# Expert loop on TensorE: one expert load per chunk, small matmuls moved inside a layer, branch prefetch hints

## Time and profile before

| what | us |
| --- | --- |
| median of 3 runs | 583.89 |
| lowest and highest of them | 580.96, 586.48 |
| the profiled execution, its own time | 583.43 |
| the span of that execution in the profile | 581.7 |
| PE busy | 569.2 (98%) |
| DVE, ACT, POOL busy | 409.2, 262.7, 177.6 |

### The profile page before, as it was taken

One profiled execution on the slowest core, in us unless ns is written; L12 is line 12 of the kernel. 1 busy time (PEld: TensorE's weight loads), 2 busy tenths in 40 slices (PEclk: granted clock), 3 DMA queues, 4 the chain that ended last, 5 costly groups with the idle time before them and its releaser, 6 DMA issues.

```text
span 581.7 us, 17023 instructions
## 1 busy us (share of the span) xinstructions
PE 569.2 (98%) x5107; PEld 501.2 (86%) x5108; DVE 409.2 (70%) x1093; ACT 262.7 (45%) x576; POOL 177.6 (31%) x529
## 2 busy tenths in 40 slices
PE   9999999999999999999999999899999998999995
PEld 5888888885889999999999999799999996866874
DVE  5969996767846686777577688755756554568766
ACT  6666757622344343435343343343435342546360
POOL 0270000000663435352524323335242500189000
PEclk9999999999999999999999999999999998999999
DMA  8712254101001223220000000000000000192322
GB/s 266 258 76 72 79 174 145 56 1 38 2 1 32 81 103 117 83 102 38 2 2 3 2 2 3 2 3 2 3 1 3 2 4 5 30 366 81 110 101 87
DMA packets 28479, 36.92 MB, mean 63 GB/s; under 512 B 4762, under 2 KB 24115, under 8 KB 28132
## 3 DMA queue, kind: packets, MB, share of 16 engines
q1 hardware_dynamic: 28292, 35.57, 18.6%
q0 software_dynamic: 96, 0.20, 0.1%
HBM read 27.30 MB, written 8.53 MB: 62 GB/s over the span
## 4 chain that ended last, share of the span: by engine, by line
PE 96%; issue 1%; DVE 1%; ACT 0%; POOL 0%; POOLq 0%; DVEq 0%
PE ps_hidden L1168 43%; PE ps_out L1196 42%; PE ps_hidden L598 4%; PE ps_hidden L647 1%; PE ps_out L618 1%; PE ps_turn L1202 1%; PE ps_out L1242 1%; PE ps_out L610 1%; PE ps_turn L631 1%; PE ps_small L631 1%; DVE X L788 1%; DVE ytmp L871 0%; PE ps_turn L1249 0%; PE ps_small L1246 0%; ACT hbuf L533 0%
## 5 line engine op out<-in xcount | busy, mean ns | idle before, releaser
L1196 PE MATMUL ps_out<-hbuf,W 128*128 128x242 f16 (+2 forms) x2304 | 250.7, 269 | 0.0
L1196 PEld LDWEIGHTS ps_out<-hbuf,W 128*128 (+1 forms) x2304 | 224.4, 98 | 18.8 <-issue 0.2
L1741 POOL COPY xs<-X 128x88 f16 x352 | 126.4, 408 | 288.5 <-PE ps_hidden L1168 179.2
L1038 ACT ACTIVATE h<-ps_hidden,b 128x242 f32<-128x242 f32 (+1 forms) x384 | 155.5, 465 | 78.8 <-PE ps_hidden L1168 78.8
L1168 PE MATMUL ps_hidden<-xs,W 128*128 128x242 f16 x1536 | 165.8, 269 | 2.1 <-issue 2.1
L1168 PEld LDWEIGHTS ps_hidden<-xs,W 128*128 x1536 | 150.4, 98 | 12.8 <-issue 2.9
L1347 DVE TENSOR_TENSOR hbuf<-h,hbuf 128x484 f16<-128x484 f32 (+2 forms) x192 | 129.8, 676 | 7.5
L1628 DVE SCALAR_TENSOR_TENSOR acc<-ytmp,wrow,acc 128x44 f32 (+1 forms) x352 | 65.8, 260 | 94.7 <-ACT ytmp L1129 90.5
L1345 DVE CAST hbuf<-h 128x484 f16<-128x484 f32 (+2 forms) x192 | 84.9, 442 | 17.8 <-ACT h L1038 16.9
L1168 PE MATMUL ps_hidden<-X,W 128*128 128x256 f16 (+1 forms) x768 | 90.3, 279 | 2.7 <-issue 2.7
L1168 PEld LDWEIGHTS ps_hidden<-X,W 128*128 128x128 f16 x768 | 75.5, 99 | 15.7 <-issue 3.8
(11 more groups left out here) (294 smaller groups left out, 305.3 us busy)
## 6 DMA issues: line engine op xcount, KB each, us to landing
stage<-in_ew SPq DMA_DIRECT2D x16, 512.0 KB, 3.8
stage<-in_xR SPq DMA_DIRECT2D x8, 512.0 KB, 3.9
moved_rows<-stage SPq DMA_DIRECT2D x8, 512.0 KB, 2.6
X<-moved_rows SPq DMA_DIRECT2D x8, 512.0 KB, 10.0
out_rows<-X SPq DMA_DIRECT2D x16, 256.0 KB, 2.2
W<-in_xT SPq DMA_DIRECT2D x7, 512.0 KB, 9.2
W<-in_fw SPq DMA_DIRECT2D x1, 2304.0 KB, 11.8
W<-in_sw SPq DMA_DIRECT2D x4, 256.0 KB, 3.4
```

The costliest lines, as they stand in the source:

```text
L1038: i = nc.scalar.activation(h32[:, j, k * size:(k + 1) * size], ps1[j][:, k * size:(k + 1) * size], ACT.Gelu_apprx_tanh, bias=b1[:, bass.ds ...
L1196: mm = pe.matmul(out, w2(e, wp, hb, db), h, start=(n == 0), stop=(n == 3 * HB - 1))
L1741: i = nc.gpsimd.tensor_copy(xs[:, parity, :, j * SEG:(j + 1) * SEG], X[:, :, bass.ds(cols[j], SEG)])
```

## The change

On TensorE only:

- `hidden_expert` gets the expert as an argument. Each step reads one expert, and the register of the chunk before is passed on to `output`, which no longer reads it again.
- `output` has a hook `between`, which is called between its two halves.
- `pack` is no longer put behind step 20 but between the two halves of the output layer of that step.
- The count is read after step 15, one parity after step 16, the other after step 17, in place of all three after step 20.
- The nest of `If` becomes an explicit chain of `br_cmp` with bodies `chunk_24`, `chunk_25` and so on. Each step from 23 on computes `min(limit - (r + 1), 1)` in a register between the two halves of its output layer and marks there a prefetch hint for the branch at its end. The register is 1 when there is a next chunk and 0 when the branch will leave. All exits go to the label `chunks_done`.

```diff
-            def hidden_expert(r, parity):
+            def hidden_expert(r, parity, e):
                 pe.wait_ge(x_staged, r + 1)
-                hidden(r + R0, expert_of(r), lambda xp, db: xs[:, parity, 2 * xp + db, 0:RC], RC)
-
-            def output(g, e, parity, size=CH):
+                hidden(r + R0, e, lambda xp, db: xs[:, parity, 2 * xp + db, 0:RC], RC)
+
+            def output(g, e, parity, size=CH, between=None):
...
                 for db in range(DB):
+                    if db == 1 and between is not None:
+                        between()
...
-            def step(r, parity):
-                hidden_expert(r, parity)
-                output(r + (R0 - 1), expert_of(r - 1), 1 - parity, RC)
+            more = pe.alloc_register("more_chunks")
+
+            def step(r, before, between=None):
+
+                e = expert_of(r)
+                hidden_expert(r, r % 2, e)
+                output(r + (R0 - 1), before, (r - 1) % 2, RC, between)
                 if r == 14:
                     key()
                 if r == 18:
                     place()
-                if r == 20:
-                    pack()
-
-            last, parity, other = expert_loops(pe, 1, step)
+                return e
+
+            def tab_value(at):
+                return pe.value_load(tab[0:1, NR * ROW + at:NR * ROW + at + 1], min_val=0, max_val=1)
+
+            e = first_expert
+            for r in range(1, NRMIN - 1):
+                e = step(r, e, pack if r == 20 else None)
+                if r == 15:
+                    count = chunk_count(pe)
+                    limit = pe.to_reg(count)
+                if r == 16:
+                    parity = tab_value(1)
+                if r == 17:
+                    other = tab_value(3)
+
+            def chunks_from(r, before):
+
+                hint = []
+
+                def chunk_ahead():
+                    pe.reg_alu(more, limit, r + 1, ALU.subtract)
+                    pe.reg_alu(more, more, 1, ALU.min)
+                    hint.append(pe.mark_branch_hint_location(more))
+
+                e = step(r, before, chunk_ahead if r + 1 < NR else None)
+                if r + 1 < NR:
+                    pe.br_cmp(limit, r + 1, f"chunk_{r + 1}", "chunks_done", "IS_GT").branch_hint(hint[0])
+                    with nc.body(f"chunk_{r + 1}", valid_engines=[mybir.EngineType.PE]):
+                        chunks_from(r + 1, e)
+
+            chunks_from(NRMIN - 1, e)
+            pe.br("chunks_done")
+            nc.switch_bb("chunks_done")
+            last = count - 1
```

More of the change, by code:

```diff
@@ L1261, in _ @@
             pe.wait_ge(r_split, 4 * E)
-            hidden_expert(0, 0)
+            first_expert = expert_of(0)
+            hidden_expert(0, 0, first_expert)
             output(NS1 - 1, SH, 1)
```

## The result

| what | before | after |
| --- | --- | --- |
| median us | 584.34 (4 runs) | 575.61 (4 runs) |
| lowest and highest | 580.96, 586.48 | 574.51, 576.93 |
| ratio, 95% interval | | 0.9868, 0.9834 to 0.9903 |
| profiled execution, its span | 583.43, 581.7 | 576.93, 575.2 |

The changed kernel is 1.3% faster; 575.2 us was forecast, in a range of 572.6 to 579.3.

What follows compares the result with a forecast made beforehand. PE was taken as the bound, with gains only in its waits for its own sequencer and the slow clock behind them. 3.98 + 0.43 + 4.30 = 8.7 us off 583.43 gave 574.7, stated as 575.2 us, range 572.6 to 579.3.

Steps and rivals of the forecast that it cites:

- What bounds the kernel: Whole kernel: PE is busy 98% of the span; no matmul is removed, so gains come from its waits, the largest 4.9 us.
- Step 20: From `pack` to the next output layer: 9.44 us become 5.46, a gain of 3.98 us, 2.3 gap and 1.7 clock.
- The conditional chunks: Eight chunks from 406.11 us: one 0.65 us read less, 0.3 us for the hint, PE bound again; gain 0.43 us.
- The end of the loop: Leaving branch of 3.56 us: hint 2.5 us ahead plus 1.8 us lead hide it, no clock drop; gain 4.30 us.
- last branch well under 1 us: Sign that the forecast is right: the branch leaving the loop, 3557 ns before, takes well under 1 us.
- What hangs on the end of the loop: All after the loop moves with its end; VectorE's chunk 21 splits finish 3.6 us early, off the path.
- A: Rival at the loop's end: the hint starts nothing, gap 1.9 us, time 578.5 us, or 577.1 without clock drop; chance 0.25.
- B: Rival in the eight conditional chunks: the hint fetches the far block instead of the next; costs 25 us, time 605; chance 0.04.
- C: Rival in the conditional chunks: read or hint is dearer, hint 1 us or more, time near 580; chance with the rest 0.09.

Runs made afterwards that it cites:

- the two kernels that undo one half each: The changed kernel with `pack` put back behind step 20, 576.75 us; the changed kernel with the three reads put back behind step 20, 577.84 us.
- the last version: The changed kernel with the hint at the top of each step and three unread 512-column matmuls in a PE wait near the end; 575.19 us, ratio 0.9835.
- the two that lost it: The changed kernel with each output layer reading its expert again, 586.78 us; the changed kernel with later PE code shifted by 94 instructions, 580.05 us.
- the late hint: The changed kernel with the hint in the middle of the output layer's second half, 12 matmuls before the branch instead of 24; 579.01 us.
- the shifted one: The changed kernel with 50 small matmuls added to the warm-up and 3 large ones removed, moving later PE code 94 instructions on; 580.05 us.

## Why the prediction was right

*What bounds the kernel.* Right. The gain came from stretches in which PE waited for its own sequencer and from the slow clock behind them; its layers keep 4.96 us.

*Step 20.* 3.98 us forecast, 3.95 measured. That `pack` costs nothing in its new place holds to 0.03 us, and the three reads cost nothing. The reason given, that four reads in a row emptied the queue, is shown by the two kernels that undo one half each. One part of this term is luck: 1.7 of the 3.98 are clock loss, which the profiled execution had and others don't. The 11 runs of the kernel before that were timed beside the last version reach from 581.96 us at a mean clock of 0.999 to 588.71 at 0.983. The forecast took one execution in the middle of this, 583.43 at 0.993. Two executions of the kernel before at a mean clock of 0.999 took 580.52 and 581.96 us, 6.0 and 7.4 us above the fastest of the changed kernel at the same clock (574.51), so without clock losses the change is worth less than the 8.7 us between the medians.

*The conditional chunks.* 0.43 us forecast and measured. The hint costs the sequencer 65 + 28 ns and not my 0.3 us. But the price of a read was taken as 0.65 us in a loop that was otherwise the same. Its removal is worth more than the old loop shows. With two reads, and the wait where it was, the sequencer takes (484.05 - 402.03) / 8 = 10.25 us for a conditional chunk of the new loop, the hint among it, against 10.04 in the old one, and the static chunks lose 1.2 us, with gaps at the spread reads.

*The end of the loop.* 4.30 us forecast, 3.48 measured. This is the term that was mis-sized. The step was "if the fetch starts at the hint and takes as long, the stall is gone whole". The fetch does start at the hint, but it takes 4.8 us until the branch is free where the branch's own took 3.56; 2.4 + 1.8 us of cover leave 0.6 open, and the first matmul starts 0.2 us later. The sign "last branch well under 1 us" did not come with it. How much is left open varies: with the reads at step 20 the same hint left no gap, and the 4.30 were had in full (483.40 to 488.80 us is 5.40). Without a hint I said 1.9 us of gap, and 2.2 were measured; the branch took 3.85 instead of 3.56.

*What hangs on the end of the loop.* VectorE's splits of chunk 21 end at 384.1, 3.3 us ahead of their output layer (3.6 forecast), and nothing else came late. What I didn't see is the clock near the end: 1.3 us lost in the profiled execution and in half of the runs. The forecast sum was 0.85 us too good in the loop. The two medians lie 8.7 us apart all the same, since clock losses in the loop, which differ from run to run, went with the gaps.

*The rivals.* A, the hint starts nothing, is not what happened here, but it is what happens when the code lies 94 instructions further on; its price, 1.9 us of gap and 1.4 of clock or none, was right within 0.35: 2.22 and 2.24 us of gap, with 1.6 us of clock in one kernel and none in the other. Of the Trainium skill's rule that prefetch is purely sequential ("Runtime: NRT & Kernel Launch", Instruction fetch mechanics) the packets of queue 8 say no: in each kernel with a hint but the two that lost it, one left that only the hint explains, ahead of the branch or, with the late hint, 0.5 us behind its start, where the branch's own take 1.0 us and more. B had the wrong price for hints at this place, as shown. C has no ground: the hint takes 28 ns.

## What to carry to other kernels

When an engine is nearly always busy, look at the lead of its sequencer: register reads cost nothing while the queue holds more time than they take, and everything when several of them meet behind short instructions. A branch out of a long unrolled loop is worth a hint, and the hint should be given as early as its outcome is known, here a whole step ahead, since it can be lost if it falls beside a block's fetch. And undo the parts of a change one by one: one read per chunk looked like 0.4 us from the old profile and carries 3.5 us in the new loop. And part of a gain that a profile shows can be clock loss that other executions of the same kernel don't have.

## What the runs showed of the hardware that I had not expected

- A fetch that a hint begins is no quicker than one that a branch begins, and mostly slower: its packet leaves 1.2 to 2.1 us behind the hint, against 1.0 to 1.6 us behind a branch, and the branch is free 3.6 to 4.8 us after the hint, against 3.6 to 3.9.
- A hint that executed about half a microsecond before the packet of the next block in sequence was lost in both cases seen; where the next packet left 1.2 us behind it, it was not. One that executed in a quiet stretch made its own fetch, and one given a whole step ahead seems to have turned the next block's fetch to the branch's target (queue 8 has 47 packets there and 48 in the changed kernel).
- Eight wrong hints cost nothing visible while the next chunk's code was there already.
- A wait for a semaphore placed ahead of a register read is carried by the read; behind the read it was an instruction of its own, and this was enough to bring the lead from 1.8 to 0.8 us over ten chunks.
- The granted clock fell to 0.50 behind gaps of 2.2 to 3.5 us in some kernels (before, without hints, two reads) and did not behind a gap of 2.2 us in the shifted one, or of 1.9 us at step 20.
